# A state-space scan stage: the residual sums go through TensorE and ScalarE, and the small chains move

## The chip, the cores and the metric

The kernel runs on one core of a Trainium2 chip. The metric is device time in microseconds (us) of one execution. Engines: PE is TensorE (PEld its weight loads), DVE is VectorE, ACT is ScalarE, POOL is GpSimd, SP is SyncE, which here only issues DMAs. Each engine works off its own queue in order and meets the others at semaphores.

## What is computed

A stack of layers over 16 sequences of 512 tokens with 128 features: two mixture-of-experts layers around an attention, then two more around a Mamba block. The change touches the Mamba block, with what enters it and what follows it:

```python
x = x + 0.5 * _L1_ffn_ref(_layernorm(x), ...)      # experts, stage c
x = x + _L1_attn_ref(_layernorm(x), ...)           # the scan stage
x = x + 0.5 * _L1_ffn_ref(_layernorm(x), ...)      # experts, stage d
# _L1_attn_ref, for 256 inner channels and 16 states
xz = W_in @ hidden;  x, z = halves of xz
xc = gate[0] * silu(conv1(x)) + gate[1] * silu(conv2(x))
dt_low, B, C = split(W_x @ xc);  delta = softplus(W_dt @ dt_low + b_dt)
h = h * exp(delta * A) + delta * B * xc            # along time
y = sum over states of h * C, + D * xc, * silu(z)
out = W_out @ y
```

## The kernel before, in words

Ten stages follow one another: load and first router, expert blocks a, attention, expert blocks b, a router, expert blocks c, the scan stage, expert blocks d, the end. X, the residual stream, stays in SBUF as 64 tiles of 128 tokens by 128 features. `scan_stage` (from line 1329) is the one that changes.

The scan stage treats one sequence of 512 tokens at a time: a **turn** s, 16 of them. Within a turn it goes through 16 **states** n; a state is one value of the state dimension for all 256 channels (two halves of 128 partitions) and 512 time steps. `state(s, n)` on VectorE is two multiplications (delta B x, into PSUM) and two `tensor_tensor_scan` instructions, lines 1796 to 1810. Around it, ScalarE makes the decays `dA = exp(delta A)` (`decay`, line 1645, three states ahead, in a ring of four), GpSimd multiplies the scanned state by C (line 1731, started once the next state's multiplications are through), and TensorE adds these products up in PSUM with identity matmuls (`total`, line 1483, two states behind).

All other work is cut into small pieces and put between the states by an order written out by hand, one loop over n for each engine: `if n == 4 and later: ...`. What this order holds is work for four sequences at once: s + 2 (`later`), s + 1 (`after`), s - 1 (`before`), s - 2 (`older`).

- For s + 2: `gather` (TensorE, psR) adds the two expert rows of each token with an identity matmul each; `take` (VectorE, `Take.dve_sum`, line 586) adds them to X; `N.dve_stats`, `N.act_root` (ScalarE: a logarithm and an exponential of 4 numbers per partition, for the inverse root), `normalize` (Newton step, from line 227) and `normal` (ScalarE, 4 instructions) make the layer norm; `flip` and `to_hT` transpose it; the first convolutions follow.
- For s + 1: the rest of the convolutions (`conv`, `empty`), the gate's projection (`conv_z`), the SiLU block (`silu`, between two table loads), `mix` and `to_xc`, `project` and `to_low`, then the step size: `steps` (TensorE), `soften` (ScalarE, first an Abs and a Relu pass for each half, then an Exp and a copy), `lengthen`, and on VectorE `correct`, `lengthen`, `weigh`. After `weigh` the next turn's states can begin.
- For s - 1: `gated` (VectorE), `out` (TensorE, 8 small products into psR), `add` (VectorE, to X), and the router of the following expert stage: statistics, root, `dve_0`, rows (`act_rows`), `logits` (TensorE transposes), the copy of the transposed rows (`R.act_1`), `R.pe_1b` (the logits themselves), `dve_2a` (maximum), `R.act_2` (exponential), `dve_2b` (choice of two experts).
- For s - 2: `places` (TensorE, small bf16 products), `dve_2c`, the scatter by GpSimd, and `act_back`.

Small VectorE chains are put into a `Between` object: `small.begin(part)` issues a chain's first instruction (and its first wait) at once, and every `small.step()` inside a state issues one more link of each open chain.

PSUM is full: psA and psR are the only two banks for everything between, psX, ux and psY serve the scan. psR holds in turn the convolution's second group, the gathered rows, the output's sum, the second mix, the router's transposes and logits and its places.

## Time and profile before

| | |
|---|---|
| Median of 3 runs | 3136.72 us (3132.16 to 3138.05) |
| The profiled execution | 3140.43 us, its span 3138.6 us |
| Scan stage, first to last scan | 1632.3 to 2753.9 us of the span |
| Mean granted TensorE clock | 0.918 |

How to read the page: the first lines give each engine's busy time over the whole span, then come 40 equal slices of 78 us, a digit for the tenths of a slice in which the engine is busy (PEclk: tenths of the full TensorE clock).

```profile
PE 2462.0 (78%) x12952; PEld 1742.6 (56%) x12952; DVE 2072.7 (66%) x6083; ACT 1591.6 (51%) x3093; POOL 1698.8 (54%) x1349
PE   4239995884799754399978888888988898759991
DVE  6414445775344455155539999999999999955553
ACT  3115554672455443255546666656666666425550
POOL 5745550455355347555515567666666667645551
PEclk9999998996899966699989999999999999879995
```

The scan stage is the run of nines in VectorE's row, slices 22 to 35. All other stages are bound elsewhere (transfers, TensorE) and are not touched.

### The profile page before, as it was taken

The page shows a single profiled execution, that of the slowest core. Times are in us where ns is not written, and L with a number is a line of the kernel's source. Part 1 is how long each engine was busy: PE and PEld are TensorE (multiplying, and loading weights), DVE is VectorE, ACT ScalarE, POOL GpSimd, SP SyncE. Part 2 cuts the span into 40 slices and gives each one's busy share as a digit, 9 for nine tenths or more (in the row PEclk, how much of TensorE's full clock was granted, in tenths as well). Part 3 has the DMA queues.
Part 4 walks back from the last instruction along what each step waited for, and adds up shares of the span by engine and source line. Part 5 has one row for each costly group of instructions (what it writes and reads, how often), then busy time and mean ns, then how long its engine had stood idle before and what let it go on. Part 6 is the DMA issues. An engine that isn't in the chain of part 4 may idle for free. (4 is left out here: it accounts for less than half of the span.)

```text
span 3138.6 us, 49074 instructions
## 1 busy us (share of the span) xinstructions
PE 2462.0 (78%) x12952; PEld 1742.6 (56%) x12952; DVE 2072.7 (66%) x6083; ACT 1591.6 (51%) x3093; POOL 1698.8 (54%) x1349
## 2 busy tenths in 40 slices
PE   4239995884799754399978888888988898759991
PEld 4239994663799633399933333333433343349991
DVE  6414445775344455155539999999999999955553
ACT  3115554672455443255546666656666666425550
POOL 5745550455355347555515567666666667645551
PEclk9999998996899966699989999999999999879995
DMA  9147771211677532477724344434334344237775
GB/s 329 53 131 229 226 224 58 69 53 41 205 228 226 159 99 78 131 229 226 216 75 142 129 134 143 140 124 136 136 124 133 135 136 145 102 114 228 226 227 170
DMA packets 268819, 479.26 MB, mean 153 GB/s; under 512 B 37453, under 2 KB 181803, under 8 KB 268560
## 3 DMA queue, kind: packets, MB, share of 16 engines
q1 hardware_dynamic: 225280, 405.41, 42.4%
q0 software_dynamic: 34816, 68.00, 6.0%
q10 hardware_dynamic: 8592, 4.33, 0.5%
q8 instruction: 54, 0.88, 0.1%
q14 instruction: 77, 0.63, 0.1%
HBM read 383.22 MB, written 98.54 MB: 153 GB/s over the span
## 5 line engine op out<-in xcount | busy, mean ns | idle before, releaser
L1731 POOL TENSOR_TENSOR ssm_HC<-ssm_H,ssm_BC 128x1024 f32<-128x1024 f32 x255 | 599.4, 2351 | 416.3 <-DVE ssm_psX L1801 329.3
L1492 PE MATMUL ssm_psY<-ssm_HC,ident 128*128 128x512 f32 x1020 | 516.9, 634 | 94.0 <-POOL ssm_HC L1731 93.8
L1650 ACT ACTIVATE ssm_dA<-ssm_delta,A 128x511 f32<-128x511 f32 x512 | 332.9, 710 | 194.0 <-DVE ssm_H L1810 133.9
L1492 PEld LDWEIGHTS ssm_psY<-ssm_HC,ident 128*128 128x128 f32 x1020 | 192.6, 198 | 363.6 <-issue 201.4
L1808 DVE TENSOR_TENSOR_SCAN ssm_H<-ssm_dA,ssm_psX 128x512 f32<-128x512 f32 x256 | 309.7, 1210 | 0.0
L1810 DVE TENSOR_TENSOR_SCAN ssm_H<-ssm_dA,ssm_psX 128x512 f32<-128x512 f32 x256 | 305.4, 1193 | 0.0
L471 POOL DMA_INDIRECT xslots<-att_r_xn,att_r_idx x128 | 128.3, 1002 | 176.6 <-DVE att_r_idx L451 138.5
L877 POOL DMA_INDIRECT b_back<-b_yr,b_to_row x144 | 139.8, 971 | 151.2 <-DVE b_yr L952 129.3
L877 POOL DMA_INDIRECT a_back<-a_yr,a_to_row x144 | 139.8, 971 | 150.4 <-DVE a_yr L952 128.4
L877 POOL DMA_INDIRECT d_back<-d_yr,d_to_row x144 | 139.8, 971 | 147.9 <-DVE d_yr L952 126.0
L877 POOL DMA_INDIRECT c_back<-c_yr,c_to_row x144 | 139.8, 971 | 143.1 <-DVE c_yr L952 119.3
L921 ACT ACTIVATE b_H<-b_psH,b_W 128x256 f32<-128x256 f32 x288 | 127.4, 473 | 125.6 <-PE b_psH L898 125.6
L921 ACT ACTIVATE d_H<-d_psH,d_W 128x256 f32<-128x256 f32 x288 | 127.4, 473 | 125.3 <-PE d_psH L898 125.3
L921 ACT ACTIVATE a_H<-a_psH,a_W 128x256 f32<-128x256 f32 x288 | 127.4, 473 | 124.4 <-PE a_psH L898 124.4
L921 ACT ACTIVATE c_H<-c_psH,c_W 128x256 f32<-128x256 f32 x288 | 127.4, 473 | 123.9 <-PE c_psH L898 123.9
L921 ACT ACT_TABLE_LOAD x72 | 92.4, 1283 | 183.4 <-PEq L162 182.2
L471 POOL DMA_INDIRECT xslots<-ssm_r_xn,ssm_r_idx x128 | 160.1, 1251 | 34.1 <-issue 23.7
L1801 DVE TENSOR_TENSOR ssm_psX<-ssm_ux,ssm_BC 128x512 f32<-128x512 f32 x256 | 176.4, 689 | 0.0
L471 POOL DMA_INDIRECT xslots<-to_c_r_xn,to_c_r_idx x128 | 125.7, 982 | 91.1 <-DVE to_c_r_idx L451 51.1
L1796 DVE TENSOR_TENSOR ssm_psX<-ssm_ux,ssm_BC 128x512 f32<-128x512 f32 x256 | 174.0, 680 | 0.6
L1428 PE MATMUL ssm_psA<-ssm_hT,Wtap 128*128 128x512 f32 x360 | 165.4, 603 | 5.4 <-ACT ssm_hT L1586 5.1
L471 POOL DMA_INDIRECT xslots<-to_a_r_xn,to_a_r_idx x128 | 125.5, 981 | 66.4 <-issue 41.0
(566 smaller groups left out, 5817.6 us busy)
## 6 DMA issues: line engine op xcount, KB each, us to landing
ssm_BC<-bc_rows SPq DMA_DIRECT2D x128, 1024.0 KB, 5.5
a_W<-in_l_pack SPq DMA_DIRECT2D x72, 514.0 KB, 3.4
b_W<-in_l_pack SPq DMA_DIRECT2D x72, 514.0 KB, 3.3
c_W<-in_l_pack SPq DMA_DIRECT2D x72, 514.0 KB, 3.4
d_W<-in_l_pack SPq DMA_DIRECT2D x72, 514.0 KB, 3.4
a_xs<-xslots SPq DMA_DIRECT2D x72, 131.0 KB
b_xs<-xslots SPq DMA_DIRECT2D x72, 131.0 KB
c_xs<-xslots SPq DMA_DIRECT2D x72, 131.0 KB
```

The source lines that it names most:

```text
L471: pool.indirect_dma_start(out=self.k.xslots[:, :], out_offset=bass.IndirectOffsetOnAxis(ap=self.ids(s, b)[:, i:i + 1].bitcast(U32), axis=0 ...
L877: pool.indirect_dma_start(out=target[:, :], out_offset=bass.IndirectOffsetOnAxis(ap=to_row[:, q, s:s + 1].bitcast(U32), axis=0), in_=yr[:, ...
L921: nc.scalar.activation(H[:, b, f, :], psH[:, f, 0:BLOCK], gelu, bias=W[:, q, HIDDEN + FT * D + f:HIDDEN + FT * D + f + 1]).then_inc(h_read ...
L1428: last = nc.tensor.matmul(out, Wtap[:, c, t, dt * P:(dt + 1) * P], hT[:, PAD - back:PAD - back + SEQ], start=(t == 0), stop=(t == TAPS - 1))
L1492: last = nc.tensor.matmul(psY[:, dt, :], k.ident[:, :], HC[:, n % RP, dt, :], start=(n == 0), stop=(n == NB - 1))
L1650: last = nc.scalar.activation(dA[:, n % RA, dt, 1:], delta[:, b, dt, 1:], ACT.Exp, scale=A[:, dt, n:n + 1])
L1731: nc.gpsimd.tensor_tensor(HC[:, n % RP, :, :], H[:, n % RH, :, :], BC[:, n // CHUNK % SLOTS, 1, n % CHUNK:n % CHUNK + 1, :].to_broadcast([ ...
L1796: nc.vector.tensor_tensor(psX[:, 0, :], ux[:, 0, :], BC[:, c % SLOTS, 0, n % CHUNK, :], ALU.mult).then_inc(dBx_half, 1)
L1801: nc.vector.tensor_tensor(psX[:, 1, :], ux[:, 1, :], BC[:, c % SLOTS, 0, n % CHUNK, :], ALU.mult).then_inc(dBx_done, 1)
L1808: nc.vector.tensor_tensor_scan(H[:, n % RH, 0, :], dA[:, n % RA, 0, :], psX[:, 0, :], 0.0, ALU.mult, ALU.add).then_inc(h_half, 1)
L1810: nc.vector.tensor_tensor_scan(H[:, n % RH, 1, :], dA[:, n % RA, 1, :], psX[:, 1, :], 0.0, ALU.mult, ALU.add).then_inc(h_ready, 1)
```

## The change

`take` and `add` leave VectorE. `gather` and `out` get one more matmul, identity times the four X tiles of the sequence, that opens the sum; ScalarE then copies the finished sum out of psR over X. In the hand-written order:

- ScalarE: `take(s + 2)` at step 1, `add(s - 1)` at step 4; `N.act_root(s + 2)` from step 4 to 6, `R.norm.act_root` 6 to 7, `normal` 6 to 8, `act_rows` 9 to 10, `R.act_1` 10 to 11; the first half of `soften` becomes `size(s, dt)` and runs at step 10, so ahead of `R.act_1`; `to_hT` goes ahead of `R.act_2`. Before the loop, `take(0)` and `take(1)` stand first in the queue.
- TensorE: `places` from step 4 to 5; `steps(s + 1, 1)` stays at step 10 and `logits` goes to step 11, `R.pe_1b` to 12.
- VectorE: statistics for s + 2 after state 2 instead of 1, for s - 1 after 4 instead of 3; `normalize` after 6 instead of 4; `dve_2c` after 6 instead of 5; `dve_0` after 8 instead of 7; `dve_2a` after 13 instead of 12; `dve_2b` after 14 instead of 13.

The diff, with unchanged lines left out:

```diff
--- before.py
+++ after.py
...
 
+        def four(s):
+            return k.X[:, s * ST:(s + 1) * ST, :].rearrange("p a d -> p (a d)")
+
         def at_least(eng, signal, count):
...
                     pe.wait_ge(emptied, s * 4 - 2)
-                G.pe(nc, pe, s, s % 2, s // 2, psR)
+                pe.wait_ge(G.arrived[s % 2], s // 2 * 16 + 16)
+                at_least(pe, G.taken, s)
+                nc.tensor.matmul(psR[:, :], k.ident[:, :], four(s), start=True, stop=False)
+                nc.tensor.matmul(psR[:, :], k.ident[:, :], G.store[:, s % 2, :, 0:D], start=False, stop=False)
+                nc.tensor.matmul(psR[:, :], k.ident[:, :], G.store[:, s % 2, :, D:], start=False, stop=True).then_inc(G.summed, 1)
 
...
                 pe.wait_ge(G.taken, min(s + 4, BATCH))
+                nc.tensor.matmul(to[:, :], k.ident[:, :], four(s), start=True, stop=False)
                 for j in range(ST):
                     for dt in range(DT):
-                        last = nc.tensor.matmul(to[:, j * P:(j + 1) * P], v[:, dt, j * P:(j + 1) * P], Wout[:, dt, :], start=(dt == 0), stop=(dt == DT - 1))
+                        last = nc.tensor.matmul(to[:, j * P:(j + 1) * P], v[:, dt, j * P:(j + 1) * P], Wout[:, dt, :], start=False, stop=(j == ST - 1 and dt == DT - 1))
                 last.then_inc(out_summed, 1)
...
                         conv(s + 1, 3, psA[:, :])
-                    if n == 4 and older:
+                    if n == 5 and older:
                         places(s - 2)
...
                         steps(s + 1, 0)
-                    if n == (10 if after else 8) and before:
-                        logits(s - 1)
                     if n == 10 and after:
...
                     if n == (11 if after else 9) and before:
+                        logits(s - 1)
+                    if n == (12 if after else 10) and before:
                         R.pe_1b(nc, pe, s - 1, 1 - b)
...
         def _(act):
+            def take(s):
+                act.wait_ge(G.summed, s + 1)
+                nc.scalar.activation(four(s), psR[:, :], ACT.Copy).then_inc(G.taken, 1)
+
+            def add(s, of=psR):
+                act.wait_ge(out_summed, s + 1)
+                nc.scalar.activation(four(s), of[:, :], ACT.Copy).then_inc(added, 1)
+
             def to_hT(s):
...
 
-            def soften(s, fronts=(psA, psA)):
-
-                for dt, front in enumerate(fronts):
-                    act.wait_ge(dt_summed, s * DT + dt + 1)
-                    nc.scalar.activation(absv[:, dt, :], front[:, :], ACT.Abs, bias=col[:, dt, 2:3]).then_inc(abs_ready, 1)
-                    nc.scalar.activation(v[:, dt, :], front[:, :], ACT.Relu, bias=col[:, dt, 2:3]).then_inc(v_half if dt == 0 else v_ready, 1)
+            def size(s, dt, front=psA):
+                act.wait_ge(dt_summed, s * DT + dt + 1)
+                nc.scalar.activation(absv[:, dt, :], front[:, :], ACT.Abs, bias=col[:, dt, 2:3]).then_inc(abs_ready, 1)
+                nc.scalar.activation(v[:, dt, :], front[:, :], ACT.Relu, bias=col[:, dt, 2:3]).then_inc(v_half if dt == 0 else v_ready, 1)
+
+            def soften(s):
                 act.wait_ge(abs_ready, s * DT + DT)
...
             act.wait_ge(setup, 1)
+            take(0)
+            take(1)
             N.act_root(nc, act, 0)
...
             to_low(0)
-            soften(0, (psA, psR))
+            size(0, 0)
+            size(0, 1, psR)
+            soften(0)
             lengthen(0)
...
                         R.act_back(nc, act, s - 2)
+                    if n == 1 and later:
+                        take(s + 2)
                     if n == 2 and after:
                         empty(s + 1, 2, psA[:, :])
-                    if n == 4 and later:
-                        N.act_root(nc, act, s + 2)
+                    if n == 4 and before:
+                        add(s - 1)
                     if n == 4 and after:
...
                         silu(s + 1, 1 - b, (psA[:, :], psA[:, :]))
-                    if n == (6 if after else 5) and before:
+                    if n == 6 and later:
+                        N.act_root(nc, act, s + 2)
+                    if n == (7 if after else 6) and before:
                         R.norm.act_root(nc, act, s - 1)
-                    if n == 6 and later:
-                        normal(s + 2)
                     if n == 7 and after:
...
                         to_low(s + 1)
-                    if n == (9 if after else 7) and before:
+                    if n == 8 and later:
+                        normal(s + 2)
+                    if n == (10 if after else 8) and before:
                         R.act_rows(nc, act, s - 1, 1 - b, (s - 1) // 2)
-                    if n == (10 if after else 8) and before:
+                    if n == 10 and after:
+                        size(s + 1, 0)
+                    if n == (11 if after else 9) and before:
                         R.act_1(nc, act, s - 1, 1 - b)
                     if n == 10 and after:
+                        size(s + 1, 1)
                         soften(s + 1)
...
                         lengthen(s + 1)
-                    if n == (12 if after else 10) and before:
+                    if n == 12 and later:
+                        to_hT(s + 2)
+                    if n == (12 if after else 11) and before:
                         R.act_2(nc, act, s - 1)
                     if n == 12 and later:
-                        to_hT(s + 2)
                         empty(s + 2, 0, psA[:, :])
...
             R.act_back(nc, act, LAST - 1)
+            add(LAST, psA)
             R.norm.act_root(nc, act, LAST)
...
 
-            def take(s):
-                G.dve_sum(nc, dve, s, psR)
+            def stats(s):
+                dve.wait_ge(G.taken, s + 1)
+                return N.dve_stats(nc, chain, s)
+
+            def restats(s):
+                dve.wait_ge(added, s + 1)
+                return R.norm.dve_stats(nc, chain, s)
 
...
                     nc.vector.tensor_tensor(HC[:, (NB - 1) % RP, dt, :], H[:, (NB - 1) % RH, dt, :], BC[:, (CHUNKS - 1) % SLOTS, 1, CHUNK - 1, :], ALU.mult).then_inc(closed, 1)
-
-            def add(s, of=psR):
-                dve.wait_ge(out_summed, s + 1)
-                four = k.X[:, bass.ds(s * ST, ST), :]
-                nc.vector.tensor_tensor(four, four, of[:, :].rearrange("p (a d) -> p a d", a=ST), ALU.add).then_inc(added, 1)
-                dve.wait_ge(added, s + 1)
 
...
             dve.wait_ge(setup, 1)
-            take(0)
-            straight(N.dve_stats(nc, chain, 0), normalize(0))
-            take(1)
-            straight(N.dve_stats(nc, chain, 1), normalize(1))
+            straight(stats(0), normalize(0))
+            straight(stats(1), normalize(1))
             correct(0)
...
                         gated(s - 1, 1 - b)
-                    if n == 1 and later:
-                        take(s + 2)
-                        small.begin(N.dve_stats(nc, chain, s + 2))
-                    if n == 3 and before:
-                        add(s - 1)
-                        small.begin(R.norm.dve_stats(nc, chain, s - 1))
-                    if n == 4 and later:
+                    if n == 2 and later:
+                        small.begin(stats(s + 2))
+                    if n == 4 and before:
+                        small.begin(restats(s - 1))
+                    if n == 6 and older:
+                        small.begin(R.dve_2c(nc, dve, chain, s - 2, b))
+                    if n == 6 and later:
                         small.begin(normalize(s + 2))
-                    if n == 5 and older:
-                        small.begin(R.dve_2c(nc, dve, chain, s - 2, b))
-                    if n == (7 if after else 5) and before:
+                    if n == (8 if after else 6) and before:
                         small.begin(R.dve_0(nc, dve, chain, s - 1, 1 - b, (s - 1) // 2))
-                    if n == (12 if after else 10) and before:
+                    if n == (13 if after else 11) and before:
                         small.begin(R.dve_2a(nc, dve, chain, s - 1, 1 - b))
...
                         lengthen(s + 1)
-                    if n == (13 if after else 11) and before:
+                    if n == (14 if after else 12) and before:
                         small.begin(R.dve_2b(nc, dve, chain, s - 1, 1 - b))
...
             straight(R.dve_2c(nc, dve, chain, LAST - 1, 0))
-            add(LAST, psA)
             clear_rows(nc, empty).then_inc(cleared, 1)
-            straight(R.norm.dve_stats(nc, chain, LAST))
+            straight(restats(LAST))
             straight(R.dve_0(nc, dve, chain, LAST, 1, LAST // 2))
```

## Rows read from the trace of the kernel before

**Rows 1.** one instruction of VectorE: count, ns min/median/max, first and last start (us).
```profile
L1767 DVE TENSOR_TENSOR ssm_ux<-ssm_delta,ssm_xc x16: 1232/1232/1234, 1629.9 to 2684.6; 128x1024 f32<-128x1024 f32 x16
```

**Rows 2.** window, one turn: length, busy us PE PEld DVE ACT POOL, PEclk, DMA, GB/s.
```profile
2122.90:2192.70 69.80, 60.78 (x174) 27.00 (x173) 68.97 (x129) 44.85 (x72) 48.34 (x25) 1.00 0.40 137
```

**Rows 3.** waits of VectorE in the scan: us in total, times, longest us.
```profile
DVE ssm_r_top L401 <- PE ssm_psR L375: 14.1, 11, 2.1
DVE ssm_r_pv L417 <- ACT ssm_r_prob L407: 8.3, 11, 1.9
DVE X L590 <- PE ssm_psR L583: 7.7, 5, 4.1
```

**Rows 4.** order of time, VectorE: start us, duration us, line, operation, operands, idle before.
```profile
1999.19 0.67 DVE L1785 TENSOR_TENSOR X<-X,ssm_psR 128x512 f32<-128x512 f32 x1
2000.01 0.87 DVE L206 BATCH_NORM_STATS2 ssm_r_stats<-X 128x6 f32<-128x128 f32 x4
```

**Rows 5.** order of time, TensorE, end of a turn.
```profile
2169.30 0.60 PE L368 MATMUL ssm_psR<-ident,ssm_r_xn 128*128 128x128 f32 x4
2171.93 1.12 PE L1466 MATMUL ssm_psA<-ssm_low,Wdt 64*128 64x512 f32 x2 [2.02 <-ACT ssm_v L1633]
2172.98 1.98 PE L1492 MATMUL ssm_psY<-ssm_HC,ident 128*128 128x512 f32 x4
2174.80 0.95 PE L375 MATMUL ssm_psR<-gate_w,ssm_r_xnT 128*128 128x8 f32 x8
```

**Rows 6.** groups by line: busy us, mean ns, idle us before and releaser.
```profile
L1586 ACT ACTIVATE ssm_hT<-ssm_psA 128x512 f32<-128x512 f32 x15 | 8.8, 586 | 4.1 <-PE ssm_psA L1412 4.1
```

**Rows 7.** order of time, VectorE, same turn: states 5 and 7, the wait-free L401.
```profile
2147.92 0.69 DVE L1796 TENSOR_TENSOR ssm_psX<-ssm_ux,ssm_BC 128x512 f32<-128x512 f32 x1
...
2155.68 0.67 DVE L1796 TENSOR_TENSOR ssm_psX<-ssm_ux,ssm_BC 128x512 f32<-128x512 f32 x1
...
2177.00 0.17 DVE L401 TENSOR_REDUCE ssm_r_top<-ssm_psR 128x4 f32<-128x32 f32 x1
```

**Rows 8.** order of time, ScalarE, same turn.
```profile
2147.91 1.33 ACT L1650 ACTIVATE ssm_dA<-ssm_delta,A 128x511 f32<-128x511 f32 x2 [3.00 <-DVE ssm_H L1810]
...
2154.74 1.33 ACT L1650 ACTIVATE ssm_dA<-ssm_delta,A 128x511 f32<-128x511 f32 x2
...
2156.21 0.21 ACT L225 ACTIVATE ssm_r_root<-ssm_r_root 128x8 f32<-128x8 f32 x1
...
2165.32 1.32 ACT L1650 ACTIVATE ssm_dA<-ssm_delta,A 128x511 f32<-128x511 f32 x2
2166.54 1.64 ACT L246 ACTIVATE ssm_r_xn<-X,ssm_r_shift,ssm_r_rstd 128x128 f32<-128x128 f32 x4
2168.08 1.32 ACT L1650 ACTIVATE ssm_dA<-ssm_delta,A 128x511 f32<-128x511 f32 x2
...
2170.62 0.68 ACT L1632 ACTIVATE ssm_pre<-ssm_psA,col 128x512 f32<-128x512 f32 x1
```

**Rows 9.** order of time, an earlier turn: `places`, gate projection, start of state 5.
```profile
2002.67 0.17 PE L440 MATMUL ssm_psR<-ssm_r_hot_bf,before 128*128 128x16 bf16 x1
...
2003.03 1.10 PE L1434 MATMUL ssm_psA<-ssm_hT,Win 128*128 128x512 f32 x2
...
2004.86 0.69 DVE L1796 TENSOR_TENSOR ssm_psX<-ssm_ux,ssm_BC 128x512 f32<-128x512 f32 x1
```

**Rows 10.** windows around a wait of TensorE, columns as in rows 2.
```profile
2028.10:2031.50 3.40, 1.38 (x7) 0.51 (x4) 3.40 (x5) 1.93 (x3) 3.03 (x3) 0.96 0.58 155
2031.50:2034.90 3.40, 3.40 (x5) 1.37 (x5) 2.52 (x3) 2.82 (x4) 3.21 (x3) 0.53 0.72 199
```

**Rows 11.** order of time, start of the stage and turn 0.
```profile
1591.59 1.88 PE L583 MATMUL ssm_psR<-ssm_t_rows,ident 128*128 128x512 f32 x4
...
1592.97 0.20 ACT L223 ACTIVATE ssm_n_root<-ssm_n_shifted 128x4 f32<-128x4 f32 x1 [7.68 <-DVE ssm_n_shifted L214]
...
1642.19 0.69 DVE L590 TENSOR_TENSOR X<-X,ssm_psR 128x512 f32<-128x512 f32 x1 [4.12 <-PE ssm_psR L583]
```

## The prediction

> **What bounds the kernel now.** I read the page first (busy shares, the 40 slices), then the waits of VectorE, one turn of the scan as a window, and last the order of time of three engines in that turn. The change touches only the scan stage, where one turn (one batch entry, 16 states) takes (2684.6 - 1629.9) / 15 = 70.3 us [rows 1]. In a turn without any low clock VectorE is busy 68.97 of 69.8 us, TensorE 60.78, ScalarE 44.85, GpSimd 48.34 [rows 2]. So VectorE's queue is the turn: what leaves it shortens the turn by its full length until another engine is late, and TensorE with 9 us to spare is the next in line. VectorE's idle time is named in its waits: 14.1 us for the router's logits (L401), 8.3 us for the router's exponentials (L417) and 7.7 us for the gathered rows before the add (L590), the longest of these, 4.1, in turn 0 [rows 3, 11]. Together 30.1 us over the stage.
>
> **Base.** The sum is made against the profiled execution (3140.43 us, span 3138.6), 3.7 us above the median of the runs shown; I carry the difference over to the median of 3136.72.
>
> **1. The two adds leave VectorE.** From the start of the add to the start of the statistics behind it 0.82 us pass, its wait on its own result included [rows 4]. L590 has the same shape and is taken at the same price. In the loop there are 14 of L590 (turns 0 to 13) and 15 of L1785 (turns 1 to 15): 29 x 0.82 = **-23.8 us**. The price is what VectorE's queue holds, so it is a saving wherever VectorE doesn't wait. A turn without waits goes from 69.0 [rows 2] to about 67.3 us. The statistics keep their time and only move.
>
> **2. What TensorE and ScalarE get for it.** TensorE: two identity matmuls of 512 columns more in each turn. The pair in a state's sum takes 2172.98 to 2174.80, so 0.9 each [rows 5]: 60.8 + 1.8 = 62.6 of 67.3 us. ScalarE: two copies of 128x512 out of PSUM at 0.59 us [rows 6], 46 of 67.3 us. Neither becomes the bound by its sum. But both are queues in order, and both are late at certain points; that decides the rest.
>
> **3. Waits that go.** The take now waits on ScalarE, behind TensorE's gather at step 0; VectorE asks for it a state later. By my count the copy is finished about 3 us before. The same for the output's add: ScalarE gives it after the decay of step 4, about 2 us before VectorE's statistics after state 4. So L590's later waits (3.6 us) go. The wait at L417 goes as well: the exponential stands behind `lengthen` and `to_hT` on ScalarE, but VectorE now asks after state 14 and its `lengthen`, a whole state and more later than before. In turn 0 the gather waits for ScalarE's early `empty`; VectorE asks 3.4 us later, the gather ends 0.9 and the copy, behind three decays, about 2 us later: 4.1 becomes about 3.0.
>
> **4. The new wait: the root behind the SiLU block.** `N.act_root(s+2)` moves from ScalarE's step 4 to step 6 and VectorE's `normalize(s+2)` from after state 4 to after state 6. In the turn of [rows 7, 8] state 5 starts at 2147.92 and state 7 at 2155.68. ScalarE starts the decay of step 5 at 2147.91, goes through two table loads and three SiLU passes, and starts the decay of step 6 at 2154.74; the root right behind it (there the router's, same two instructions) ends at 2156.42. So a root given there is ready 8.5 us after state 5 starts, and VectorE, with fewer small instructions in states 5 and 6, asks about 7.5 us after. That is 1.0 us. On top, TensorE is later against VectorE in this place: before, the gate's projection started at 2003.03 and was through 0.7 us before state 5 began at 2004.86 [rows 9]; now two identity matmuls (+1.8) stand ahead, VectorE is 2 x 0.82 us earlier, and `places`, 2002.67 to 2003.03, has left: about 2.4 us after state 5 begins. ScalarE needs it only after a decay and a table load, so it nearly hides; I add 0.3 for what doesn't (`empty(s+1, 3)` ahead of the decay, the gate's second half). I take **1.3 us** in each of the 14 turns that have `later`: **+18.2 us**. Bounds: 0.8 without the lag, 2.9 where a stretch of low clock (below) falls on TensorE's backlog. Nothing is queued between; behind the waiting VectorE instruction stand state 7 and all after it.
>
> **5. The router's logits (L401).** In the same turn [rows 5, 7, 8], had the rest stayed: ScalarE would leave `to_low` at 2165.32, then `normal` (1.54), decay (1.22), decay (1.24), the router's rows (1.54), first step-size passes (1.31 from 2170.62 to TensorE's answer at 2171.93). TensorE's second step-size matmul starts at 2172.2; its state's sum before it ends at 2169.3, so it idles 2.9 us where it idled 2.0. Then 1.05 + 1.82 for a state's sum + 0.5 transposes + 1.8 diagonal + 1.8 sum + 0.95 logits: finished at 2180.1. VectorE asks after state 13, one state of 3.4 us past 2177.0: 2180.4. It fits with 0.3 us; before it fitted with 1.2. The wait of step 4 moves VectorE, not this chain, later by 1.3: slack 1.6 us. What can take it is the clock. With TensorE busy 1.38 of 3.4 us (2.0 of it the wait for ScalarE) the next stretch runs at a granted clock of 0.53, near the lower of the levels 1.2 and 2.4 GHz [rows 10]; that stretch loses 3.4 x (1 - 0.53) = 1.6 us of work. L401 waited in 11 turns, 2.1 us at the longest [rows 3]: a slack of 1.2 less one such loss is a wait of 0.4, less two a wait of 2.0. The longer idle makes a loss likelier. One is covered by the new slack, two are not: I take 1.2 us too much in three turns, some **+3.5 us**, bounds 0 and 20.
>
> [...]
>
> **6. Outside the loop.** Start: ScalarE takes both first takes ahead of `N.act_root(0)`. The second gather started at 1591.59 and the root at 1592.97 [rows 11]. Now the gather starts 0.9 later and takes 2.6, ending at 1595.1; copy and signals 0.8: root at 1595.9, **+2.9 us**, with nothing beside it, since VectorE's first state waits for this chain. End: the last output sum is 0.9 longer on TensorE, the add of 0.82 leaves VectorE: +0.1.
>
> **Sum.** -23.8 - 30.1 + 3.0 (turn 0) + 18.2 + 3.5 + 2.9 + 0.1 = **-26.2 us**: 3114.2 for the profiled kind of run, **3110.5** on the median.
>
> **Rivals.**
> (a) *No new wait.* ScalarE is early enough at step 6, or the root's pair is faster there, and the clock holds. For it: L401 fits with 0.3 us even alone, and the more loaded TensorE idles less before the mix. Against: the 8.5 us of [rows 7, 8] are ScalarE's own instructions. -23.8 - 30.1 + 3.0 + 2.9 = -48.0: **3088.7**. [...]
> (b) *The lag is paid in full.* A low stretch falls into TensorE's backlog between the gather and the gate's projection in most turns, so SiLU and root come 1.6 us later: 2.9 x 14 = 40.6 in place of 18.2 and 3.5: -7.3, **3129.4**.
> (c) *The small chains only change places.* The root's 1.3 and a wait for logits of the old kind (2.1, the longest of before) add up in every turn: 3.4 x 14 = 47.6: -0.3, **3136.4**. In this case the adds' saving is real and the turn gives it back; it is also how the change could fail to do what it says. Against: the first wait gives the second chain slack.
> (d) *TensorE becomes the bound* (slower). Its turn is 62.6 busy + 2.9 waiting for ScalarE = 65.5, plus 1.6 per low stretch. From three such stretches in each turn it decides over VectorE's 70.3; at four, 71.9, the 14 turns cost 22 us and the start 3: **3162**. For it: 62.6 us plus the wait leave under 2 us of 67.3. Against: before, whole turns ran at clock 1.00 [rows 2], and a busier TensorE has shorter gaps elsewhere.
>
> **How the numbers follow.** A difference under 0.2% (6.3 us) can't be told from no change here. Chances: forecast 0.53 (its own range 3100 to 3121), (a) 0.19, (b) 0.16, (c) 0.07, (d) 0.05. (b) straddles the 6.3 us bound: a fifth of it counts as no change. Faster 0.85, same 0.10, slower 0.05. The range runs from (a)'s value, 3088, to (b)'s, 3130: it leaves out (c), (d) and the rim of (a) and (b).
>
> **What would show it.** Right: no VectorE record at L590 or L1785; a turn of about 69 us; a wait of VectorE at the norm's Newton step (L232, n_newton) for ScalarE's root, about 1.3 us, 14 times; L417's waits gone; L401's in few turns. The first ScalarE logarithm 2.9 us later. Step 4 is wrong if L232 shows no wait, step 5 if L401 waits in most turns; then TensorE's idle time before the second step-size matmul (I say 2.9 us) tells whether chain or clock did it. The prediction fails as a whole if VectorE shows a new wait for dA (ScalarE's decays late) or for the summed y (TensorE late), for I gave both nothing.

## The result, and the profile after

The change makes the kernel slower: 3150.19 us, median of 7 runs (3147.93 to 3152.18), against 3136.72 us before (7 runs), a ratio of 1.0047 with an interval of 1.0038 to 1.0056. I had forecast 3110.5, range 3088 to 3130. The profiled execution took 3152.18 us, its span 3150.3, 11.7 more than the span before. By the start times of `ux` (now L1801) those 11.7 us are: 15 turns of the scan +6.7 (1054.7 to 1061.4 us), the start of the stage +7.3, and all else -2.3. The stage's first matmul itself came 4.2 us later, before any changed code, so only the rest, 3.1, can belong to the change. In another execution of the changed kernel (**again** below) the turns start at 1630.0 and take 1063.8 us: the start of the whole stage varies by more than the change adds to it, and the longer turns are what comes again.

The page's first line, and the changed kernel's row that answers to [rows 1]:

```profile
PE 2507.6 (80%) x13016; PEld 1766.4 (56%) x13016; DVE 2048.1 (65%) x6051; ACT 1611.1 (51%) x3125; POOL 1689.6 (54%) x1349
```
```profile
L1801 DVE TENSOR_TENSOR ssm_ux<-ssm_delta,ssm_xc x16: 1232/1233/1234, 1637.2 to 2698.6; 128x1024 f32<-128x1024 f32 x16
```

The mean turn is 70.76 us (before 70.31). But the turns have another shape. Before, the thirteen between the first and the last (67.0 and 67.1) scatter between 69.4 and 71.8. After, the eleven from the fourth to the fourteenth are 71.67 to 71.78 us, as if copied. The waits of VectorE in the scan, to be read beside [rows 3] (us in total, times, longest us):

```profile
DVE ssm_n_newton L232 <- ACT ssm_n_root L225: 39.8, 14, 3.7
DVE ssm_r_top L401 <- PE ssm_psR L375: 17.5, 12, 1.5
DVE ssm_v L1807 <- PE ssm_psY L1500: 4.3, 14, 0.7
```

L590 and L417 are gone, as meant. In their place stands a wait for the root in 14 turns, and the logits' wait has grown instead of vanishing: 61.6 us in these three rows against 30.1 before (0.7 of the last row falls behind the fifteenth turn). In one of the equal turns the waits are 2.82 (L232), 1.46 (L401) and 0.24 (L1807). Without them the turn would be 71.68 - 4.52 = 67.16 us.

One such turn cut at the changes of TensorE's clock (length; busy us of PE, PEld, DVE, ACT, POOL with counts; PEclk; DMA share; GB/s), as [rows 2, 10]. It begins shortly before `ux` at 2202.41:

```profile
2201.00:2207.70 6.70, 4.47 (x12) 1.73 (x10) 6.63 (x10) 5.29 (x9) 4.44 (x3) 0.98 0.03 11
2207.70:2211.10 3.40, 3.40 (x5) 1.48 (x6) 3.31 (x6) 3.13 (x7) 3.27 (x2) 0.53 0.72 243
2211.10:2248.60 37.50, 35.72 (x107) 16.04 (x106) 34.53 (x81) 23.10 (x38) 19.72 (x10) 1.00 0.36 117
2248.60:2252.00 3.40, 1.27 (x4) 0.37 (x3) 3.40 (x7) 3.03 (x7) 3.10 (x3) 0.98 0.69 230
2252.00:2258.80 6.80, 6.80 (x11) 2.91 (x12) 6.80 (x9) 4.80 (x7) 6.39 (x5) 0.51 0.58 175
2258.80:2272.70 13.90, 13.90 (x43) 6.86 (x42) 12.44 (x18) 6.83 (x9) 10.37 (x6) 1.00 0.47 166
```

There are two low stretches, 3.4 us at 0.53 and 6.8 us at 0.51, near the lower of 1.2 and 2.4 GHz. TensorE had worked only part of the time before each fall, and is busy without a gap in each. They cost 3.4 x 0.47 = 1.6 and 6.8 x 0.49 = 3.3 us of work. They recur 71.7 us later and again after that. The order of time on TensorE around the first (start us, us, line, operation, idle before):

```profile
2207.62 3.60 PE L1500 MATMUL ssm_psY<-ssm_HC,ident 128*128 128x512 f32 x4 [2.23 <-POOL ssm_HC L1760]
2211.05 1.02 PE L1411 MATMUL ssm_psR<-X,ident 128*128 128x512 f32 x2
...
2223.14 3.60 PE L1435 MATMUL ssm_psA<-ssm_hT,Wtap 128*128 128x512 f32 x8
```

TensorE waits 2.23 us for GpSimd's `HC` of the turn before; then the last sum of that turn takes 3.4 us instead of the usual 1.7, and everything queued behind it (gather, convolutions, gate projection) stays 1.6 us late. ScalarE, same turn:

```profile
2226.77 0.69 ACT L1607 ACTIVATE ssm_pre<-ssm_psA,col 128x512 f32<-128x512 f32 x1 [4.06 <-PE ssm_psA L1435]
...
2234.27 1.33 ACT L1666 ACTIVATE ssm_dA<-ssm_delta,A 128x511 f32<-128x511 f32 x2
2235.51 0.19 ACT L223 ACTIVATE ssm_n_root<-ssm_n_shifted 128x4 f32<-128x4 f32 x1
2235.72 0.21 ACT L225 ACTIVATE ssm_n_root<-ssm_n_root 128x4 f32<-128x4 f32 x1
```

`empty(s+1, 3)` waits 4.06 us for the fourth convolution. Decay, SiLU block, decay and root stand behind it in ScalarE's queue. VectorE meets both waits:

```profile
2235.96 0.16 DVE L232 SCALAR_TENSOR_TENSOR ssm_n_newton<-ssm_n_root 128x4 f32<-128x4 f32 x1 [2.81 <-ACT ssm_n_root L225]
...
2262.89 0.19 DVE L401 TENSOR_REDUCE ssm_r_top<-ssm_psR 128x4 f32<-128x32 f32 x1 [1.46 <-PE ssm_psR L375]
```

The second low stretch lies on the logits' chain. It follows TensorE's wait for ScalarE's step-size passes, and the state's sum behind that takes 3.78 us:

```profile
2251.82 2.07 PE L1473 MATMUL ssm_psA<-ssm_low,Wdt 64*128 64x512 f32 x2 [2.13 <-ACT ssm_v L1647]
2253.82 3.78 PE L1500 MATMUL ssm_psY<-ssm_HC,ident 128*128 128x512 f32 x4
...
2261.90 0.95 PE L375 MATMUL ssm_psR<-gate_w,ssm_r_xnT 128*128 128x8 f32 x8
```

**Theory.** The root's place behind the SiLU block costs a wait by itself. On top, TensorE's low stretches fall on the same two places in every turn, where each delays a chain that VectorE waits for. **Rivals:** that the root's wait merely takes the place of another (undoing it then gives nothing); that TensorE is the bound; that either half of the change alone is at fault.

### The profile page after: what moved, and what is told of

Read it like the earlier page. It is cut to its first block and busy times, and to the rows that moved or that the text cites. A ratio compares the mean times of both kernels' runs of the same rounds, so it can differ in the third digit from the quotient of the medians.

```text
span 3150.3 us, 49201 instructions
## 1 busy us (share of the span) xinstructions
PE 2507.6 (80%) x13016; PEld 1766.4 (56%) x13016; DVE 2048.1 (65%) x6051; ACT 1611.1 (51%) x3125; POOL 1689.6 (54%) x1349
## 5 line engine op out<-in xcount | busy, mean ns | idle before, releaser
L1500 PE MATMUL ssm_psY<-ssm_HC,ident 128*128 128x512 f32 x1020 | 531.0, 651 | 76.4 <-POOL ssm_HC L1760 75.6
L471 POOL DMA_INDIRECT xslots<-ssm_r_xn,ssm_r_idx x128 | 150.7, 1178 | 34.7 <-issue 21.9
```

Source lines behind the costliest of these rows:

```text
L471: pool.indirect_dma_start(out=self.k.xslots[:, :], out_offset=bass.IndirectOffsetOnAxis(ap=self.ids(s, b)[:, i:i + 1].bitcast(U32), axis=0 ...
L1500: last = nc.tensor.matmul(psY[:, dt, :], k.ident[:, :], HC[:, n % RP, dt, :], start=(n == 0), stop=(n == NB - 1))
```

## The experiments

Beside the first and third group of runs below, the kernel before took 3313.16 and 3318.77 us, as against 3134.6 beside the second. Nearly all that is added lies ahead of the scan (the first `ux` starts at 1795 to 1804 instead of 1630 to 1638), and some 12 us behind it; why is open, for the second and third group ran on one chip. So ratios are taken within a group, and only turns are set side by side across them. The mean turn before, 70.31, stands for one execution of the second kind.

### First group: one part undone, or one part alone

**root4.** The changed kernel, with the root back on step 4 of ScalarE and its Newton step behind state 5.

```
 # ScalarE
-                    if n == 6 and later:
+                    if n == 4 and later:
                         N.act_root(nc, act, s + 2)
...
 # VectorE
-                    if n == 6 and later:
+                    if n == 5 and later:
                         small.begin(normalize(s + 2))
```

> The changed kernel with one move undone: the root of the layer norm for s + 2 goes back to ScalarE's step 4, ahead of the SiLU block, and the Newton step on VectorE begins after state 5. Theory ADD (the root wait of 2.8 us is time of its own): that wait goes, the logits' wait stays about 1.5, turn 68.9 us, time 3150 - 39 = 3111 us. Rival MAX (the chain from TensorE's backlog through SiLU, mix and step size to the logits sets the turn, and VectorE waits for it wherever it asks first): the logits' wait grows by what the root's loses, 1.5 to about 4.3, turn stays near 71.7, time 3145 to 3152 us.

Measured: ratio 0.988 (0.9859 to 0.9902), mean turn 67.6 us; no wait for the root is left. The waits of VectorE in the turns:

```profile
DVE ssm_r_top L401 <- PE ssm_psR L375: 10.8, 5, 4.6
DVE ssm_v L1807 <- PE ssm_psY L1500: 1.0, 2, 0.7
```

Eight of the turns are 67.4 to 67.6 us, about VectorE's content. The wait for the root is a cost of its own: undoing this one move takes 47.4 us off the 15 turns (1061.4 to 1014.0), more than the 39.8 of the wait itself, for the logits' wait falls too. TensorE is not the bound: it has kept both X matmuls.

**fill.** The changed kernel with two matmuls that nobody reads ahead of each of TensorE's two waits. They only keep it busy. `keep_busy` is two identity matmuls of 512 columns into psA or psR; the first filler waits until ScalarE has emptied psA.

```
+                        if after:
+                            pe.wait_ge(emptied, s * 4 + 5)
+                            keep_busy(psA, 2)      # first filler
                         total(s - 1, 1 - b, NB - 1)
...
+                        keep_busy(psR, 2)          # second filler
                         steps(s + 1, 1)
```

> The changed kernel plus filler matmuls on TensorE inside its two longest waits of a turn: two of 512 columns before the last sum of the turn before, two before the second step-size matmul. Theory CLOCK (in the changed kernel the granted clock falls after these two waits, at the same two places of each turn, and the slow stretches make SiLU, root and logits late): the clock stays up, VectorE's wait for the root falls from 2.8 to about 1.2 us, that for the logits from 1.5 to under 0.3, turn 71.7 to about 68.7 us, time about 3150 - 42 = 3108 us. Rival QUEUE (TensorE's queue is simply too long between the gather and the gate projection, whatever the clock): fillers sit in idle time, waits stay at 2.8 and 1.5, time 3145 to 3155, or longer where a filler delays what stands behind it.

Measured: 0.9973 (0.9954 to 0.9993), mean turn 69.01, eight of the turns at 68.93 to 68.96. L401 no longer waits in the turns; the root's wait stays, 31.6 us in 14, mostly 1.54. It is 3.24 in four turns, 70.6 to 71.0 us long, and these are the four with a low stretch of 3.4 us, 6.3 to 6.6 us behind `ux`. So 2.8 splits into 1.5 that is there with the clock up and 1.3 that belongs to the clock, and the logits' wait is the clock's. The turns came out as expected, the time didn't: 0.9973 is 0.6% above the 3108 us I had set down, and the turns, at 69.01 instead of 68.7, make only some 5 us of that. In the profiled execution the first `ux` starts at 1804.1, in the other three of this group at 1795.4 to 1796.4, and the runs spread over 3294.55 to 3313.46.

**moves_only** and **adds_only** part the change in two. The first keeps both adds on VectorE, without the X matmuls and ScalarE's copies, but moves all small chains as the change does. The second has the adds on TensorE and ScalarE, and the chains on their old steps (only the two statistics come a state later, since X does).

```
 # moves_only
-                nc.tensor.matmul(to[:, :], k.ident[:, :], four(s), start=True, stop=False)
+                    if n == 1 and later:
+                        take(s + 2)                # VectorE adds
 # adds_only
-                    if n == 6 and later:
+                    if n == 4 and later:
                         N.act_root(nc, act, s + 2)
```

> Half of the change: every chain at its new step, but take and add stay VectorE adds where they were (after states 1 and 3), and TensorE has no identity matmul for X. If the moves alone did the harm (root behind SiLU), VectorE waits 1.0 us or more for the root in 14 turns and the time is over before's 3137, about 3140 to 3155. If the moves help and the X matmuls with ScalarE's copies do the harm, root wait under 1.2, logits' wait near 0, exponential's gone: before - 8 to - 20, so 3117 to 3129 us.

> The other half: take and add on TensorE and ScalarE as in the change, the two statistics one state later since they need the copies, all other chains (roots, Newton steps, router's chain, step-size passes, places) at the steps of before. If the adds' removal is real and the root at step 4 is harmless: -24 us of VectorE work, the logits' wait grows by part of it since VectorE arrives 1.6 us earlier (up to 1.6 x 14 = 22): 3112 to 3138 us. If TensorE's 1.8 us more per turn are the cause by themselves, 3145 us or more with waits for logits over 3 us.

Measured: moves_only 0.9988 (0.9971 to 1.0006), mean turn 69.48; adds_only 0.9912 (0.9895 to 0.9928), mean turn 67.73. Their waits, first moves_only, then adds_only:

```profile
DVE X L590 <- PE ssm_psR L583: 8.3, 7, 3.3
DVE ssm_r_top L401 <- issue: 5.1, 3, 1.7
DVE ssm_n_newton L232 <- ACT ssm_n_root L225: 2.1, 2, 1.7
```
```profile
DVE ssm_r_pv L417 <- ACT ssm_r_prob L407: 8.8, 14, 1.5
DVE ssm_v L1805 <- PE ssm_psY L1500: 2.7, 14, 0.4
```

("issue" means that the profile shows nothing that the instruction waited for; the same wait of 1.6 us stands once more with TensorE named.)

Neither half is slow. With the adds still on VectorE the wait for the root is there in two turns instead of 14; with the root still on step 4 the adds' saving stays whole. What joins the two shows at the decay ahead of the SiLU block. First a turn of moves_only with `ux` at 2003.90, then one of fill with `ux` at 2216.84:

```profile
2027.31 1.33 ACT L1653 ACTIVATE ssm_dA<-ssm_delta,A 128x511 f32<-128x511 f32 x2 [1.70 <-DVE ssm_H L1824]
```
```profile
2239.58 0.69 ACT L1611 ACTIVATE ssm_pre<-ssm_psA,col 128x512 f32<-128x512 f32 x1 [2.79 <-PE ssm_psA L1435]
2248.78 0.16 DVE L232 SCALAR_TENSOR_TENSOR ssm_n_newton<-ssm_n_root 128x4 f32<-128x4 f32 x1 [1.54 <-ACT ssm_n_root L225]
```

In both the root starts 31.7 us behind `ux`. In moves_only ScalarE was held by VectorE's own scan, and VectorE is free for the Newton step at 31.8. In fill, with the clock up, ScalarE is held by TensorE's fourth convolution, and VectorE, without its adds, is there at 30.4: the 1.4 us it has gained it spends waiting. The changed kernel's whole loss needs both halves. But moves_only doesn't clear the root's move: that one move alone costs 1.05 us per turn with the adds on VectorE (root6_alone, below). There VectorE asks 7.5 us after this decay starts, in moves_only 8.4, since the change's other moves put the statistics (0.84 us) in between.

adds_only also has twelve turns of 68.25 to 68.27 us, each with one low stretch, which begins about as far behind `ux` (5.2 us in the rows below) as the first one of the changed kernel does (5.3). In one turn of adds_only:

```profile
2130.64:2135.80 5.16, 1.20 (x3) 0.19 (x1) 5.12 (x8) 5.16 (x9) 3.19 (x2) 1.00 0.04 13
2135.80:2139.20 3.40, 3.34 (x4) 1.31 (x5) 3.40 (x6) 3.18 (x7) 3.15 (x3) 0.55 0.64 237
2139.20:2198.91 59.71, 57.69 (x169) 26.50 (x168) 59.05 (x114) 37.23 (x59) 41.82 (x22) 1.00 0.43 146
```

No wait for the root and hardly one for the logits (0.2 us, once) stands behind these stretches. So equal turns and a low stretch do little harm by themselves. They do when a chain without slack stands behind them.

### Second group: both cures, one filler, and a shift

**again.** The changed kernel once more.

> The changed kernel as it is, so that it shares a chip and its runs of the kernel before with the experiments. If the slowdown belongs to the scan stage, its turns are again about 71.7 us long with waits of 2.8 us for the root and 1.5 us for the logits, and the ratio to before is 1.003 to 1.006.

Measured: 3151.11 us, 1.0048 (1.0033 to 1.0064); all turns but the first two and the last are 71.61 to 71.71 us, with the same three waits. The equal turns are a property of the kernel and not of one execution. Equal turns alone don't show that the clock sets them, though: root4_fill, the next run, has eleven of 67.39 to 67.42 us without a low stretch in any. What is special here is that the stretches come back at the same distance behind `ux`.

**root4_fill.** root4 and both fillers.

> Both remedies on the changed kernel: root back at ScalarE's step 4, fillers in TensorE's two long waits. If clock and root position are the two causes and nothing stands behind them, every turn falls to VectorE's own content, 67.2 to 67.5 us: against root4 (67.6 on the mean, four turns at 67.7 to 70.8) 3 to 6 us less, ratio to before about 0.986. If the fillers delay the sums behind them (TensorE is busy 91% of a turn), waits of VectorE for the summed y show and it is slower than root4, ratio 0.99 or more.

Measured: **3090.32 us, 0.9848 (0.9825 to 0.987)**, the fastest version. Its waits in the turns, and one whole turn:

```profile
DVE ssm_n_stats L206 <- ACT X L1598: 1.4, 1, 1.4
```
```profile
2101.06:2168.47 67.41, 63.95 (x183) 28.83 (x182) 67.34 (x127) 45.56 (x75) 48.10 (x25) 1.00 0.41 142
```

VectorE works 67.34 of 67.41 us. TensorE has as much to do as in fill and more than in any other version, and that costs nothing. Beside root4 (0.9859 to 0.9902, on another chip) the intervals overlap, so the ratios don't show the fillers' gain; in the mean turn it is 67.6 to 66.9 us, one profiled execution each.

**fill0.** The changed kernel with the first filler alone.

> The changed kernel with the fillers only in the first of the two waits (before the last sum of the turn before). Theory TWO PLACES: the low stretch there goes, so the root's wait falls from 2.8 to 1.5 us, and the low stretch before the logits stays, so their wait stays or grows by what the root's loses (1.5 to 2.8). Turn 70.4 to 71.7. If one place drives both, the logits' wait goes as well and the turn is 69 us, as with both fillers.

Measured: 3118.07 us, 0.9939 (0.9918 to 0.996); mean turn 68.8. Its waits:

```profile
DVE ssm_n_newton L232 <- ACT ssm_n_root L225: 24.9, 14, 3.6
DVE ssm_r_top L401 <- PE ssm_psR L375: 4.4, 3, 1.5
```

One filler of two matmuls takes 33 us off the changed kernel (3151.11 to 3118.07 in this group). So it was the second of the two expected outcomes, one place drives nearly all of it. TensorE still waits 2.12 us before the second step-size matmul, but the low stretch behind it is 3.4 us long in nine of the twelve turns from the third to the fourteenth, and 6.8 us only in three; these three are the turns in which L401 waits. Where and for how long the clock falls depends on more than the last wait. What sets this I leave open. The root instruction starts 31.71 us behind `ux` instead of 33.31, the 1.6 us of the lost stretch.

**delay.** The changed kernel with 0.48 us of useless work for VectorE (a fill of 128x512) in each of 15 turns, ahead of the next turn's first state.

```
                         lengthen(s + 1)
+                        nc.vector.memset(idle[:, :], 0.0)
```

> The changed kernel with a VectorE memset of 512 elements (some 0.3 to 0.5 us) added behind the pass of state 14, past both waits, in 15 turns. Theory LOCK (the ten turns of 71.68 to 71.69 us are alike because the low stretches of TensorE's clock hold the turn to a length; work on VectorE is taken out of its waits): turn stays at 71.69, waits shrink by the memset. Rival PLAIN (waits are measured from the start of a turn and nothing corrects them): each turn longer by the memset, 72.0 to 72.2, together 5 to 8 us, waits unchanged.

Measured: 3153.18 us, 1.0055 (1.0038 to 1.0073). Its waits:

```profile
DVE ssm_n_newton L232 <- ACT ssm_n_root L225: 43.5, 14, 4.9
DVE ssm_r_top L401 <- PE ssm_psR L375: 10.1, 7, 1.5
```

The equal turns are gone (70.54 to 72.8 us from the third to the fourteenth), and the mean turn rises from 70.92 (again, same group) to 71.08: 2.4 us in 15 turns for 7.2 us of added work, no more than two executions of the changed kernel differ (1061.4 and 1063.8). On the mean neither value came out that I had set down. But from the eighth turn on they repeat in threes, 72.48, 70.55 and 72.02 us, and these have a mean of 71.68, the changed kernel's turn to the hundredth. Over the fourth to the fourteenth turn the mean is 71.68 in both again and delay. So in these turns the added work cost nothing at all; the logits' waits are shorter by 7 us for it. The loop keeps its mean length against half a microsecond of work, as the theory LOCK had it, though not turn by turn, and the shift doesn't bring a good phase either.

### Third group: the rest of the factors

**root6_alone.** The kernel before, with nothing but the root and its Newton step moved to where the change puts them (and `normal` two steps behind).

> The kernel before with one move alone: the root of the layer norm for s + 2 at ScalarE's step 6 behind the SiLU block, its Newton step on VectorE after state 6, and the normalising pass at step 8. By step 4 of the prediction the root is ready 8.5 us after state 5 begins and VectorE asks 7.5 to 7.9 us after: a new wait of 0.6 to 1.0 us in 14 turns, 8 to 14 us, of which the logits' wait gives back up to the same since VectorE comes there later: time equal to before up to +10 us. If the wait is 1.5 us as in the changed kernel with the clock held, ScalarE's lag there is the move's own; if under 1.0, it comes from TensorE's identity matmuls for X.

Measured: 1.003 (1.0014 to 1.0046), mean turn 70.57. Its waits, to be read beside [rows 3]:

```profile
DVE ssm_n_newton L232 <- ACT ssm_n_root L225: 15.8, 14, 1.7
DVE X L590 <- PE ssm_psR L583: 9.0, 7, 3.1
DVE ssm_r_top L401 <- PE ssm_psR L375: 6.2, 5, 1.6
DVE ssm_r_pv L417 <- ACT ssm_r_prob L407: 1.4, 3, 0.8
```

The move alone brings 1.05 us in twelve of the turns, against the 1.0 of the prediction's step 4. Beside [rows 3], L401 and L417 have lost 7.9 + 6.9 us and L590 has gained 1.3. There the wait mostly changes places and costs a little on balance: the first rival of the theory holds for the kernel before, and fails for the changed one (root4). That it is 1.05 and not 1.5 answers what I had asked of this run in part only: the change adds to the root's wait even with the clock up.

**no_x.** The changed kernel without the two X matmuls; the residual X is left out of both sums.

> The changed kernel without the two identity matmuls for X (X is left out of both sums, the copies stay; so the residual is missing from the result). Theory BACKLOG (the 1.7 us of matmuls between the last sum of the turn before and the third convolution are what makes SiLU and root late): the root's wait falls from 2.8 to 1.3 us or less and the logits' with the clock; turn 67.4 to 69.5, time 20 us or more under the changed kernel. Rival (root position and clock alone): wait stays over 2, turn over 70.5.

Measured: 0.9942 (0.9921 to 0.9963), mean turn 68.6:

```profile
DVE ssm_n_newton L232 <- ACT ssm_n_root L225: 21.3, 13, 3.4
DVE ssm_v L1805 <- PE ssm_psY L1498: 2.7, 8, 0.4
```

Some 26 us less work (29 pairs of matmuls at 0.9, as in [rows 5]) for an engine that idles 6 us of each turn saves 1.0% (1.0047 to 0.9942, from two groups), about 33 us; the 15 turns are 32.4 us shorter. What counts is not TensorE's sum but when it reaches the convolution and the logits. The run parts backlog and clock only in part, though: the low stretch at the logits is never 6.8 us long here, and L401 doesn't wait. At the root the wait fell from 2.82 us to between 1.0 and 1.5 in most turns, though a stretch of 3.4 us lies ahead of them, and is 2.2 to 2.4 in the three turns where that stretch lasts 6.8 us. So a stretch of 3.4 us hides, at least in part, when TensorE has the two X matmuls less to do.

**before_fill0** and **root4_fill0** put the first filler alone into the kernel before and into root4.

> The kernel before with the filler matmuls before the last sum of the turn before. Does the filler help without the change? Before had low stretches there in few turns, most after the wait for the step-size pass. If that filler also keeps these away, as in the changed kernel, the logits' wait (14 us over the stage) falls under 6 and the time by 8 to 14 us, ratio 0.996 to 0.997; if not, the ratio is 1.000 and the filler's gain exists only with the change.

> The best version so far with the fillers before the step-size matmul left out. If the first place drives both low stretches, as the run with this filler alone suggests, turns stay at 67.4 us and the ratio at 0.985; if the second filler has a part of its own, some turns show a logits' wait of 1.5 to 2.8 us and the ratio is 0.987 to 0.989.

Measured: before_fill0 0.9997 (0.9985 to 1.0009), mean turn 69.89 against 70.31; root4_fill0 0.9902 (0.9883 to 0.992), mean turn 67.72, no better than root4's 67.6. In root4_fill0 every other turn from the fourth to the fourteenth is 69.1 us, and L401 is what is left (one more wait of 2.1 has no releaser in the profile):

```profile
DVE ssm_r_top L401 <- PE ssm_psR L375: 12.9, 6, 2.6
```

With the root on step 4 the first filler removes every low stretch near `ux` and gives nothing, since no chain without slack stands behind that place; the seven turns of 69.1 us or with an L401 wait are those with a stretch of 6.8 us at the logits. In the kernel before it doesn't even remove them: four turns have a low stretch some 6 us behind `ux`, as many as without the filler. So before_fill0 doesn't test what such a cure would be worth there. Only the second filler clears the logits, for root4_fill shows no L401 at all in its turns.

## Why the prediction was wrong

**Step 1 held.** Content of a turn without waits 67.3 forecast, 67.16 found.

**Step 2 held, TensorE's sum a little high.** ScalarE 46 forecast, 46.18 in the whole turn. TensorE 62.6 forecast at the full clock; a turn of root4 without a low stretch (2200.1 to 2267.5) has 61.35. The 62.23 in the turn of adds_only has a low stretch in it. In the changed kernel it is 65.55, because two stretches run at half the clock.

**Step 3 held by its letter.** L590 and L417 don't appear, and the wait in turn 0 is 1.4 us, less than the 3.0 I gave it.

**Step 4 is the term that failed by most.** Its mechanism was right and its size wrong. I gave the root 1.3 us, bounds 0.8 and 2.9: 18.2 us in all. It is 1.54 with the clock kept up (fill) and 2.82 as the kernel runs: 39.8 us, 21.6 more. The upper bound was the case that came, the condition of rival (b), to which I gave 0.16. I had read that condition as an accident of single turns, but the stretch fell there in every turn from the fourth on. Of the 2.82, the place by itself is 1.05 (root6_alone; I had 1.0), the rest that stays with the clock up 0.5 (I had 0.3) and the clock 1.3 (which I had in the upper bound only). The rows were at hand, for TensorE had both idle times before, the first of them at 5.2 us behind `ux` in most turns, 2.8 to 4.0 us long:

```profile
PE ssm_psY L1492 <- POOL ssm_HC L1731: 93.8, 53, 4.0
PE ssm_psA L1466 <- ACT ssm_v L1633: 28.3, 14, 2.0
```

**Step 5 failed as well.** I forecast 3.5 us at L401 with bounds of 0 and 20, and 17.5 came, 14.0 more. By my own sign, a wait in most turns, the step was wrong. TensorE's idle time ahead of the second step-size matmul is 2.13 us, not 2.9, so by the test that I had set it was the clock and not ScalarE's chain, and fill confirms it. The low stretch there is 6.8 us long in just the twelve turns that wait, a loss of 3.3 us against a slack of 1.6. I had counted on three turns. Both terms counted the low stretches as rare, and that count is what failed.

**Step 6 held.** The stage's first matmul before, then the same and the first logarithm after:

```profile
1584.42 3.51 PE L1400 MATMUL ssm_psY<-Wtap,ident 128*128 128x512 f32 x4 [9.55 <-DVE ssm_r_run L455]
```
```profile
1588.60 3.78 PE L1403 MATMUL ssm_psY<-Wtap,ident 128*128 128x512 f32 x4 [9.55 <-DVE ssm_r_run L455]
...
1600.31 0.20 ACT L223 ACTIVATE ssm_n_root<-ssm_n_shifted 128x4 f32<-128x4 f32 x1
```

With [rows 11] it was 1592.97 - 1584.42 = 8.55 us, and is 1600.31 - 1588.60 = 11.71: +3.2 against +2.9. In again it is 11.17, +2.6.

**The sum.** Forecast for the turns: -23.8 - 30.1 + 3.0 + 18.2 + 3.5 = -29.2. Found: the adds still give about -24, and the old waits -30, but the new ones give back 39.8 + 17.5 + 4.3 + 1.4 = 63.0, which makes some +9 (8 without the 0.7 behind the fifteenth turn); the turns show +6.7. My argument against rival (c), that a wait for the root gives the logits' chain slack, is true of VectorE and should have been worth 2.8 us here; I take it that the low stretches ate it (1.6 us ahead of the convolution, 3.3 at the logits), but no run shows these parts one by one. So (b) and (c) came at once, and I had priced them only as alternatives: 39.8 and 17.5 belong in one sum. I had also given the summed y (now L1807) nothing, which I had named as a sign that the prediction fails, and it took 4.3 us.

**The sign** hung on that. No rival of mine that was slower than before was the true one: (d), TensorE as the bound, is refuted by root4_fill, where TensorE works 63.95 us in a turn of 67.41. root4 alone stands at 0.988 x 3136.72 = 3099 us and root4_fill at 3090.32, near rival (a)'s 3088.7, which had the root's wait away and the clock up: the adds' move was worth what I had said, and the root's move, with the clock's falls, was what spent it.

## What to carry to other kernels

When an add leaves the engine that bounds a loop, the engine that takes it gets later in its queue, and whatever reads that queue gets a deadline it didn't have; move the small chains behind such a reader only where their slack is larger than that lag plus one low stretch of the clock. In a periodic loop price a low stretch also as falling on the worst place in every turn, not only in some, and add the waits of different chains instead of letting the largest stand for all. If a chain must stand behind TensorE's idle time, two matmuls that nobody reads can be cheaper than the idle time: 33 us here for 15 turns, and nothing where the chain has slack (root4_fill0).

## What the runs showed of the hardware

- TensorE's granted clock fell to about 0.5 though the engine had worked 1.27 of the 3.4 us before, and stayed there for 6.8 us in which it was busy without a gap.
- Two identity matmuls of 512 columns ahead of TensorE's wait for GpSimd removed the fall behind it in every turn of fill0 and root4_fill0. In fill it stayed in four turns, and in the kernel before it came as often as without them (four turns).
- The loop fell in step with these stretches: eleven turns of 71.67 to 71.78 us in one execution and twelve of 71.61 to 71.71 in another, each with its stretches at the same distance behind `ux`. 0.48 us more on VectorE made three turns of different lengths out of it, which repeat with the same mean, 71.68 us. The equal turns of adds_only (68.26 us, one low stretch of 3.4) are 3.4 us shorter. Why the loop settles on such lengths wasn't settled; that the low stretches shift the waits which cause them is argued, not shown.
